# TensorE's attention step moves between a unit's down and up products

## The reference

```python
x = x + attn(cond(x))          # cond: softmax pooling over the sequence by prompt type
                               # attn: 16 heads of 8, latent K/V, rotary part of 32, causal
x = x + ffn(cond2(x))          # cond2: one of 64 matrices per sequence; ffn: 64 experts
# ffn, for every token, with w_dense from a top-8 routing in 4 of 8 groups:
for wg, wu, wdn, cw in zip(We_gate, We_up, We_down, w_dense.T):
    y += cw[:, None] * ((silu(x @ wg) * (x @ wu)) @ wdn)
y += silu(x @ Ws_gate) * (x @ Ws_up) @ Ws_down
```

## Time and profile before

| | us |
|---|---|
| three runs | 736.17, 2394.43, 736.21 |
| median of the runs | 736.21 |
| the profiled execution, its own time | 734.65 |
| its span from the first to the last instruction | 732.8 |

### The profile page before, as it was taken

How to read it: one execution, slowest core, us unless ns; L and a number is a source line. 1 busy time by engine, 2 the same in 40 slices (tenths; PEclk the granted TensorE clock), 3 DMA queues, 4 the chain that set the end, 5 groups by cost and what they waited for, 6 DMA issues and landing times.

```text
span 732.8 us, 15746 instructions
## 1 busy us (share of the span) xinstructions
PE 706.5 (96%) x5616; PEld 544.9 (74%) x5616; DVE 543.8 (74%) x1146; ACT 445.1 (61%) x857; POOL 424.5 (58%) x351
## 2 busy tenths in 40 slices
PE   7889899999999999999999999999999999999997
PEld 6666687677877778777787777777787777887885
DVE  4777769777697777886688866976778876876664
ACT  2877765576546855567455675557654675555553
POOL 2537686864465645565456644556455664566665
PEclk9999999999999999999999999999999999999999
DMA  7335774344543454445434353444344344444441
GB/s 267 89 118 153 220 135 125 103 125 133 116 134 103 132 117 117 132 108 151 108 111 120 121 152 105 129 106 139 103 129 138 91 151 111 109 129 141 127 133 44
DMA packets 66845, 92.93 MB, mean 127 GB/s; under 512 B 7888, under 2 KB 26768, under 8 KB 66768
## 3 DMA queue, kind: packets, MB, share of 16 engines
q1 hardware_dynamic: 61728, 85.90, 42.9%
q10 hardware_dynamic: 5040, 6.03, 2.5%
HBM read 88.37 MB, written 3.15 MB: 125 GB/s over the span
## 4 chain that ended last, share of the span: by engine, by line
PE 71%; DVE 12%; ACT 9%; issue 3%; POOL 3%; DMA 2%; SPq 0%; POOLq 0%; ACTq 0%; DVEq 0%
PE banks L992 68%; DVE act_w L959 4%; POOL hid_lo L637 2%; DVE hid L971 2%; ACT s_t L402 2%; ACT hid_hi L540 2%; ACT banks L528 1%; ACT L528 1%; PE banks L1072 1%; ACT L402 1%; DMA x_early<-in_x_feat 1%; DVE head_max L712 1%; DVE s_t L711 1%; ACT v_blk L389 1%; DMA cwb<-cw_scratch 1%
## 5 line engine op out<-in xcount | busy, mean ns | idle before, releaser
L637 POOL TENSOR_TENSOR hid_lo<-hid,hid_hi 128x512 fp32r<-128x512 f32 (+1 forms) x264 | 342.1, 1296 | 267.2 <-ACT hid_hi L540 265.4
L959 DVE TENSOR_TENSOR act_w<-banks,cwb 128x512 f32<-128x512 f32 x254 | 174.6, 687 | 127.5 <-ACT banks L528 121.5
L528 ACT ACTIVATE banks<-banks 128x512 f32<-128x512 f32 x254 | 147.3, 582 | 139.4 <-PE banks L992 136.8
L540 ACT CAST hid_hi<-hid 128x512 fp32r<-128x512 f32 (+1 forms) x264 | 162.6, 616 | 73.4 <-DVE hid L971 71.7
L971 DVE TENSOR_TENSOR hid<-act_w,banks 128x512 f32<-128x512 f32 (+1 forms) x264 | 181.3, 687 | 24.0 <-PE banks L992 1.4
L992 PE MATMUL banks<-c_hi,wg_hi 128*128 128x512 f32 x264 | 118.1, 447 | 2.9 <-DVE act_w L959 2.1
L992 PE MATMUL banks<-hid_hi,wd_hi 128*128 128x512 f32 (+1 forms) x264 | 107.0, 405 | 4.3 <-POOL hid_lo L637 4.0
L992 PE MATMUL banks<-hid_hi,wd_lo 128*128 128x512 f32 (+1 forms) x264 | 103.9, 393 | 0.0
L992 PE MATMUL banks<-c_lo,wg_hi 128*128 128x512 f32 x264 | 103.8, 393 | 0.0
L992 PE MATMUL banks<-hid_lo,wd_hi 128*128 128x512 f32 (+1 forms) x264 | 103.8, 393 | 0.0
L992 PE MATMUL banks<-c_hi,wg_lo 128*128 128x512 f32 x264 | 103.7, 393 | 0.0
(11 more groups left out here) (159 smaller groups left out, 798.4 us busy)
## 6 DMA issues: line engine op xcount, KB each, us to landing
cwb<-cw_scratch SPq DMA_DIRECT2D x254, 256.0 KB, 3.8
k_blk<-in_cond_w SPq DMA_DIRECT2D x112, 64.0 KB, 2.5
xf<-in_x_feat SPq DMA_DIRECT2D x8, 256.0 KB, 3.8
out_feat<-y ACTq DMA_DIRECT2D x8, 256.0 KB, 3.4
wg_raw<-in_we_gate SPq DMA_DIRECT2D x7, 256.0 KB, 4.6
wu_raw<-in_we_up SPq DMA_DIRECT2D x7, 256.0 KB, 4.7
wd_raw<-in_we_down SPq DMA_DIRECT2D x7, 256.0 KB, 4.9
xf<-in_x_tok SPq DMA_DIRECT2D x6, 256.0 KB, 2.7
```

What stands on the lines that cost most here:

```text
L528: nc.scalar.activation(dst, gate_bank(p)[:, :], ACT.Silu).then_inc(S["silu_done"], 1)
L540: nc.scalar.copy(hid_hi[0:n, p % NH, :], hid[0:n, p % NH, :]).then_inc(S["hi_ready"], 1)
L637: nc.gpsimd.tensor_sub(hid_lo[0:n, p % NH, :], hid[0:n, p % NH, :], hid_hi[0:n, p % NH, :].bitcast(F32)).then_inc(S["lo_ready"], 1)
L959: nc.vector.tensor_mul(act_w[:, p % NH, :], gate, weight)\
```

## The change

On TensorE, a unit's attention step is emitted between down and up instead of behind up. Units 0 and 1 of the first block keep their order. No other engine's list is changed, and no wait is added or removed.

```diff
                 elif prev:
                     down(b - 1, UNITS + p - NH)
+                between = prev or p >= 2
+                steps = steps_in(p, following, last)
+                if between:
+                    for step, blk in steps:
+                        attention_step(step, blk)
                 if p < NPAIR:
...
                     three(up_bank(p)[:, :], wu_hi[:, p, :], wu_lo[:, p, :], c_hi[par][:, :], c_lo[par][:, :], True, True)\
                         .then_inc(S["up_done"], 1)
-                steps = steps_in(p, following, last)
                 if not prev and p == 0:
                     value_products(1)
-                    steps = []
                 elif not prev and p == 1:
                     attention_step(5, 1)
                     first_weights()
-                for step, blk in steps:
-                    attention_step(step, blk)
+                    for step, blk in steps:
+                        attention_step(step, blk)
```

## The result

The changed kernel takes **750.67 us** (median of 749.17 to 752.74); the kernel before took 736.17 beside it. The ratio is **1.0202, 95% interval 1.0181 to 1.0223**, so the change makes the kernel 14.5 us slower; that it is slower is clear, whether by more than 2% is not. Three executions on record were in a slow state and stand in no comparison: two of the kernel before (2394.43 and 2927.82 us) and one of an experiment's kernel (838.18 us). The forecast was 747.0 with a range of 741 to 756: the sign is right, the time lies in the range, and 3.7 us are missing from the sum. The profiled execution after is the longest of its runs, 752.74 us with a span of 750.9 and a mean granted clock of 0.987 (before: 734.65, 732.8 and 0.993).

The account below looks back on a forecast made before the run. TensorE was taken to set the pace. Five full blocks at 1.60 us (8.0), the seventh at 1.26 and the first at 1.4 gave 10.7 us; on 734.65, plus 1.56 to the median, 747 us, range 741 to 756.

Parts of the forecast that it names:

- Unit 0, -0.27: Start of a block: value products and rotary scores cover TensorE's wait ahead of up, 0.27 us gained a block.
- Unit 3, +1.04: Step 8 starts when it did, up(3) queues behind it and gate(4) comes later: 1.04 us lost a full block.
- Units 5 to 9, +0.14: Chain to the table load and unit 9's down product about 0.9 us later, mostly already counted: 0.14 us more a block.
- Ups not swallowed: Rival: TensorE arrives last at unit 9, so up(7) and up(8) add up to 1.4 us a block: 757 us; chance 0.15.
- Unit 12, +0.50: Step 17 waits for VectorE's last `att`, which up(12) hid before: 0.50 us lost a full block.
- Units 14 and 16, +0.19: Steps 19 and 21 wait for a VectorE sum behind hid: 0.19 us lost together in a full block.
- The first block, 1.4: Units 0 and 1 keep their order; later units lose, up(8) finds room in a wait: 1.4 us more.
- Not slower: Rival: an earlier step brings the chain into unit 9 forward, 0.9 us gained a block: 730 us; chance 0.05.
- the rival on the clock: Longer wait in unit 3 lowers TensorE's clock, 1.7 us in each of seven blocks: 759 us; chance 0.05.

## Why the prediction was nearly right

- **Unit 0, -0.27**: 0.25 in the fifth block of the changed kernel (0.15 to 0.32 in the second to the seventh), and 0.20 to 0.33 a block where it alone is moved.
- **Unit 3, +1.04**: the sum worked out hid(1), `y`, step 8, gate(4) and hid(3) at 7.39, 9.31, 12.75, 14.64 and 14.84 us into the block. They came at 7.37, 9.30, 12.75, 14.64 and 14.84.
- **Units 5 to 9, +0.14**: the table load came 0.93 later (0.9 worked out), the down product of unit 9 0.95 (0.9). Gate(10) then starts 1.07 later; 0.10 of this is the restart that now stands ahead of it, and 0.97 is left where 0.91 was forecast. *Ups not swallowed* is ruled out by the kernel that moves units 7 to 11 alone.
- **Unit 12, +0.50**: 0.50 in the rows of the transposes, 0.55 from gate(12) to gate(13), 0.58 with what units 10 and 11 add.
- **Units 14 and 16, +0.19**: 0.33 in the fifth block; the sum's own terms, 0.14 and 0.04, make 0.18. This and the small excesses above make 1.9 a full block instead of 1.6.
- **The first block, 1.4**: 1.8, too uncertain to tell apart. *Not slower* is out: the table load came later, as the sum said.

The step that failed is the rival on the clock: a chance of 0.05, and a price that was all or nothing, 1.7 us in each of seven blocks. What happened lies between, 1.3 to 1.4 us in some of the blocks. By the medians: the order costs 10.8 us in six blocks and 1.8 in the first; of the 14.5 that leaves about 1.9 for the clock, a fall or two in a run, while the profiled execution with its three falls lost 4.2. It is an estimate by difference, and no surer than the 1.8 (0.4 to 2.9) in it. That 1.9, and 1.9 from terms mis-sized by a few hundredths up to 0.4, are the missing 3.7. The prediction had the row that should have raised the chance: a wait of 2.15 us in the first block with a fall behind it, and its own sum put a wait of nearly that length into seven blocks. The time lies within the sum's bounds of 742 to 754 as well, but these have no term for the clock: for that half of the excess the hit is luck.

It stays open what decides in which blocks the clock falls: waits of 1.22 had a fall in six blocks of six in one execution, waits of 1.52 to 1.57 in three of six in another. In the first block with unit 3 in the old order, step 8 started 1.82 and 1.89 us behind the matmul before it without a fall (before, and with units 7 to 11 moved), and 1.89 and 1.66 with one (with unit 12, and with unit 0 moved). A hint stands in the trace of the kernel with unit 3 alone: the six falls begin at 160.30, 249.04, 337.79, 426.54, 515.28 and 604.03 us, 88.74 to 88.75 apart, while the blocks take 88.30 to 89.03; those of the changed kernel begin at 160.94, 249.69 and 515.93, 88.75 and three times 88.75 apart. So the falls keep a beat of their own, and where a wait lies on it may decide; no run tests that. In which order, if any, the first block's loads could be kept from swallowing a gain was not tried.

## What to carry to other kernels

When a consumer is moved ahead of a producer on an in-order engine, follow the delayed producer, not the advanced consumer: here every loss came from an up product that was queued behind a waiting step and from the VectorE work behind it. Where a step waits for another engine, moving it later, behind more independent work, can remove the stop that moving it earlier doubles. And a wait of TensorE that grows (here from 0.91 to 1.92 us) has to be priced twice, once as itself and once as a chance of a slower clock behind it.

## What the runs showed of the hardware

- The low clock comes behind the wait, not in it: 1.00 over 157.30 to 160.70 with TensorE busy for 1.83 of 3.40 us, then 0.52 with TensorE busy throughout.
- Five additional matmuls of 128x512 in the wait, 1.33 us of TensorE's time, cost nothing and kept the granted clock at 1.00 in all six blocks of the profiled execution, though a stop of 0.35 to 0.44 remained.
